# Layer norm of the first layer shared between two engines, small weights loaded later

## What is computed

```python
def reference(L0_attn_x, ...):
    x = x + 0.5 * ffn(layernorm(x), gate_W, w1_e, w3_e, w2_e, w1_s, w3_s, w2_s)   # layer 1
    x = x + attn(layernorm(x), w_qkv, w_swiglu, w_out)
    x = x + 0.5 * ffn(layernorm(x), ...)                                          # layer 2
```

## Time and profile before

| | |
|---|---|
| median of 3 executions | 735.5 us (734.17 to 737.56) |
| span of the profiled execution | 733.5 us |
| TensorE busy | 660.3 us, 90% |
| VectorE busy | 458.8 us, 63% |
| ScalarE busy | 411.3 us, 56% |
| GpSimd busy | 430.6 us, 59% |

### The profile page before, as it was taken

How to read it: one execution, slowest core, us unless ns; L and a number is a source line. 1 busy time by engine, 2 the same in 40 slices (tenths; PEclk the granted TensorE clock), 3 DMA queues, 4 the chain that set the end, 5 groups by cost and what they waited for, 6 DMA issues and landing times.

```text
span 733.5 us, 14294 instructions
## 1 busy us (share of the span) xinstructions
PE 660.3 (90%) x4860; PEld 602.1 (82%) x4860; DVE 458.8 (63%) x1177; ACT 411.3 (56%) x861; POOL 430.6 (59%) x511
## 2 busy tenths in 40 slices
PE   3878999999999999957987777999999999999995
PEld 3767879999999999825654574888999999999983
DVE  6678895554445555359999867884555555544536
ACT  2658617666666666236654436664666666666520
POOL 5600075777777776489987424007577777777530
PEclk9989999999999999989999997999999999999999
DMA  9542011221222231131100002402212212212137
GB/s 296 231 78 40 1 42 38 56 52 52 52 55 52 52 53 44 57 105 44 47 12 1 0 1 46 73 2 49 40 55 54 52 52 56 51 53 52 43 104 261
DMA packets 35685, 45.91 MB, mean 63 GB/s; under 512 B 6432, under 2 KB 27936, under 8 KB 35232
## 3 DMA queue, kind: packets, MB, share of 16 engines
q1 hardware_dynamic: 25632, 24.39, 11.8%
q0 software_dynamic: 9984, 20.63, 11.5%
HBM read 28.41 MB, written 16.58 MB: 61 GB/s over the span
## 4 chain that ended last, share of the span: by engine, by line
PE 65%; DVE 20%; issue 4%; ACT 4%; POOL 3%; DMA 2%; SPq 1%; ACTq 0%; POOLq 0%; DVEq 0%
PE psY L1487 18%; PE psG L1334 6%; PE psU L1336 6%; PE psG L1336 6%; PE psU L1335 6%; PE psG L1335 6%; PE psU L1334 6%; PE psH L1405 4%; DVE rec L1076 3%; PE psT L1433 2%; DVE hs L748 2%; DVE XN L738 2%; DVE ln_stats L725 1%; DVE xn L1060 1%; POOL results L641 1%
## 5 line engine op out<-in xcount | busy, mean ns | idle before, releaser
L626 POOL DMA_INDIRECT rows<-tokens,source x156 | 153.7, 985 | 156.3 <-DVE source L900 98.6
L1155 ACT ACTIVATE silu<-psG 128x512 f32<-128x512 f32 x220 | 131.1, 596 | 150.6 <-PE psG L1336 147.2
L954 DVE TENSOR_TENSOR hT<-silu,psU 128x512 f32<-128x512 f32 x156 | 107.4, 688 | 158.9 <-PE psU L1336 150.3
L641 POOL DMA_INDIRECT results<-yout,target x156 | 153.8, 986 | 63.3 <-issue 45.7
L1487 PE MATMUL psY<-W,hT 128*128 x1232 | 162.4, 275 | 1.8 <-DVE yout L980 1.8
L1487 PEld LDWEIGHTS psY<-W,hT 128*128 128x128 f32 x1232 | 150.4, 191 | 2.2 <-DVE hT L954 2.2
L1229 ACT ACTIVATE w_high<-W13H 128x1024 fp32r x78 | 82.7, 1061 | 59.0 <-PE psU L1336 54.8
L1334 PE MATMUL psG<-xTH,w_high 128*128 128x256 f32 x312 | 100.0, 321 | 0.7 <-ACT w_low L1229 0.7
L1336 PE MATMUL psG<-xTH,w_low 128*128 128x256 f32 x312 | 88.0, 282 | 0.0
L1336 PE MATMUL psU<-xTH,w_low 128*128 128x256 f32 x312 | 88.0, 282 | 0.0
L1335 PE MATMUL psU<-xTL,w_high 128*128 128x256 f32 x312 | 87.7, 281 | 0.0
(11 more groups left out here) (188 smaller groups left out, 1215.7 us busy)
## 6 DMA issues: line engine op xcount, KB each, us to landing
W<-w_e SPq DMA_DIRECT2D x3, 2048.0 KB, 13.7
tokens<-XN SPq DMA_DIRECT2D x16, 260.0 KB, 5.9
Y<-results SPq DMA_DIRECT2D x32, 128.0 KB, 2.2
YF<-results SPq DMA_DIRECT2D x16, 256.0 KB, 5.9
rows<-tokens,source POOLq DMA_INDIRECT x156
results<-yout,target POOLq DMA_INDIRECT x156, 2.3
X<-x SPq DMA_DIRECT2D x8, 256.0 KB, 5.5
out<-X SPq DMA_DIRECT2D x8, 256.0 KB, 2.8
```

Of the source, the lines that this page charges most:

```text
L626: pool.indirect_dma_start(rows[:, slot(l, g), t, :], None, tokens, bass.IndirectOffsetOnAxis(ap=source[:, tile:tile + 1], axis=0))\
L641: pool.indirect_dma_start(results, bass.IndirectOffsetOnAxis(ap=target[:, tile:tile + 1], axis=0), yout[:, g % 2, t, :], None).then_inc(y_ ...
L954: dve.tensor_tensor(hT[:, s.u // PT % 2, half, :].rearrange("p f c -> p (f c)"), silu[:, s.u % 2, :], psU[:, s.u % 2, :], ALU.mult).then_i ...
L1155: act.activation(silu[:, s.u % 2, :], psG[:, s.u % 2, :], ACT.Silu).then_inc(silu_done, 1)
```

## The change

Three things change, all for layer 1 only. VectorE normalises the first two of a chunk's four tiles, and ScalarE the other two as `Identity(scale * x + bias)`, with `ln_rstd` as scale and a new `ln_shift = -mean * rstd` as bias. For that VectorE makes `ln_minus` (minus the mean, one more small operation in each `stats`) and GpSimd multiplies it by `ln_rstd` (one more small operation in each `scale_ln`). The small weights are issued behind the fourth transfer of `X` in place of the second. TensorE no longer waits for `small_in` ahead of its first transpose but ahead of its first gate product, and ScalarE makes `W13SH` at c = 3 in place of first. The core of the diff:

```diff
+LN_DVE = CH // 2
@@ SyncE
-                if c == 1:
+                if c == 3:
                     for dst, src in ((GATE[:, :], gateT), (W13S[:, 0, :], w1_s), (W13S[:, 1, :], w3_s),
@@ SyncE, keep_tokens
+                    if l == 0:
+                        sp.wait_ge(xn_half_done, s.i + 1)
@@ GpSimd, scale_ln
                 pool.wait_ge(ln_stat, s.i + (l * CHUNKS + 1))
+                if l == 0 and s.i >= 2:
+                    pool.wait_ge(xn_half_done, s.i - 1)
                 pool.tensor_tensor(ln_rstd[:, s.u, :], ln_var[:, s.u, :], minus_half[:, 0:CH], ALU.pow)\
                     .then_inc(ln_scaled, 1)
+                if l == 0:
+                    pool.wait_ge(ln_scaled, s.i + 1)
+                    pool.tensor_tensor(ln_shift[:, s.u, :], ln_minus[:, s.u, :], ln_rstd[:, s.u, :], ALU.mult)\
+                        .then_inc(ln_shifted, 1)
@@ VectorE, stats
+                if l == 0:
+                    if s.i >= 2:
+                        dve.wait_ge(ln_shifted, s.i - 1)
+                    dve.tensor_scalar(ln_minus[:, s.u % 2, :], ln_mv[:, s.u % 2, :, 0], -1.0, None, ALU.mult)
@@ VectorE, normalise
-                for t in range(CH):
+                for t in range(LN_DVE if l == 0 else CH):
@@ ScalarE
-                if l == 0:
+                def normalise_half(c):
+
+                    act.wait_ge(ln_scaled, c + 1)
+                    act.wait_ge(ln_shifted, c + 1)
+                    for t in range(LN_DVE, CH):
+                        i = act.activation(XN[:, c * CH + t, 0:D], X[:, c * CH + t, :], ACT.Identity,
+                                           scale=ln_rstd[:, c % 2, t:t + 1], bias=ln_shift[:, c % 2, t:t + 1])
+                    i.then_inc(xn_half_done, 1)
+
+                def split_shared():
                     act.wait_ge(small_in, 64)
                     act.activation(W13SH[:, :, :], W13S[:, :, :], ACT.Copy).then_inc(ws_high, 1)
                 if l == 0:
+                    normalise_half(0)
                     for c in range(CHUNKS + 2):
+                        if c == 3:
+                            split_shared()
+                        if c < CHUNKS - 1:
+                            normalise_half(c + 1)
                         if c < CHUNKS:
                             copy_xnT(Step.of(c, 2))
@@ TensorE
             pe.wait_ge(consts, CONSTS)
-            pe.wait_ge(small_in, 64)
@@ TensorE, ahead of the transposes of chunk c
                         pe.wait_ge(xn_done, CHUNKS * l + c + 1)
+                        if l == 0:
+                            pe.wait_ge(xn_half_done, c + 1)
@@ TensorE, ahead of the gate products of chunk c - 1
                         pe.wait_ge(xnT_done, CHUNKS * l + c)
+                        if l == 0 and c == 1:
+                            pe.wait_ge(small_in, 64)
```

More of the change, by code:

```diff
@@ L225, in macaron @@
         ln_rstd = sb("ln_rstd", [P, 2, CH])
+        ln_minus = sb("ln_minus", [P, 2, CH])
+        ln_shift = sb("ln_shift", [P, 2, CH])
         row_a = sb("row_a", [P, TILES])
@@ L367, in macaron @@
         ln_scaled = sem("ln_scaled")
+        ln_shifted = sem("ln_shifted")
         xn_done = sem("xn_done")
+        xn_half_done = sem("xn_half_done")
         xnT_psum = sem("xnT_psum")
```

## The result

The changed kernel takes 736.26 us (median of 20 executions, 734.17 to 738.19) against 734.96 us of the kernel before (20 executions, 733.47 to 737.56). The ratio is 1.0021, with a 95% interval of 1.0011 to 1.0030: 1.5 us more (0.8 to 2.2); the two medians themselves lie 1.3 us apart. It was forecast as 736.4 us, within 0.5% of no change. Its profiled execution spans 735.0 us against 733.5.

The account below looks back on a forecast made before the run. The front up to `hs(3)` was taken to bound the kernel, with T(7) passing shifts on one to one. T(7) +1.3 us, or +0.45 with an earlier upper clock, gave +0.9: 734.4 span, 736.4 us median, range 733.5 to 739.5.

Parts of the forecast that it names:

- The stall on X: VectorE's 1.7 us wait for the third chunk of X, behind 832 KB of small weights, was to go.
- ScalarE's half: Two normalises per chunk on ScalarE: 0.6 us of its time, 0.7 to the end, table load of 1.28 moved to 7.0.
- `W13SH` at c = 3: GpSimd's `low_shared` waits for it ahead of `scale_ln(4)`, putting the power of chunk 4 at 19.5, 2.5 us later.
- s: The start of `W13SH` on ScalarE behind `XNTH(0)`, forecast at 15.98 us.
- GpSimd the bound at 2.65 us a chunk: From c = 4 on, power, small product and `XNTL` were to give GpSimd a 2.65 us period, against 2.42 before.
- the port: A GpSimd `XNTL` holds up VectorE's `tensor_scalar` until it ends; with this rule ignored, +0.95 us in place of +1.3.
- The clock: TensorE without early gaps might reach its upper level sooner, L(1) ending 0.85 us earlier: +0.45 in place of +1.3, taken as +0.9.
- rival B: TensorE's idle stretch lowers its clock for c = 5 to 7; slower only from the second step; 738.5 to 740.6 us; chance 0.18.
- Sum: 733.5 + 0.9 = 734.4 us of span, plus 2.0 us to the median: 736.4 us, +0.1%.
- Rival C: ScalarE's `normalise_half(7)` between `silu(0)` and `silu(1)` costs two table loads, +1.3 to +2.6 us, 737.7 to 739 us; chance 0.1.
- Rival A: The front's gain comes through if GpSimd and ScalarE meet `W13SH` sooner, -0.9 to 0, 734.6 to 735.5 us; with D 0.22.

Follow-up runs that it names:

- e1: The changed kernel with `W13SH` made on ScalarE at c = 1 in place of c = 3; ratio to the kernel before 0.9979.
- e10: The changed kernel with VectorE normalising all four tiles (no half on ScalarE) and `W13SH` made at c = 1; ratio to the kernel before 0.9977.
- e2: The changed kernel with only the order of transfers and waits changed, VectorE normalising all four tiles; ratio to the kernel before 1.0050.
- e5: The changed kernel with 22 unused products of constants on TensorE ahead of its wait for chunk 4; ratio to the kernel before 1.0025.
- e6: e1 with unused products of constants on TensorE, 9 ahead of the wait of chunk 4 and 4 ahead of chunk 5; ratio to the kernel before 0.9974.
- e9: The changed kernel run and profiled once more, unaltered; ratio to the kernel before 1.0017.
- e8: e1 with GpSimd's `XNTL` one chunk later in layer 1, behind the power of chunk 5; ratio to the kernel before 0.9962.
- e7: e2 with 23 unused products of constants on TensorE ahead of the wait of chunk 4; ratio to the kernel before 1.0049.
- e11: e8 with `normalise(7)` ahead of `hs(0)` on VectorE and `normalise_half(7)` ahead of `silu(0)` on ScalarE; ratio to the kernel before 0.9964.

## Why the prediction was right, point by point

**The stall on X goes, and VectorE gets ahead.** Right: no wait for X, `stats(2)` at 7.41; `ln_var(4)` in the forecast at 12.8, in the trace at 12.74. The third X landed at 6.75, not 5.4, still 0.7 us ahead of its use.

**ScalarE's half.** The size was at my upper bound, not in the middle: one instruction with two pointers took 0.482 us, a pair 0.88 to its end (I took 0.7, the bound was 0.87). The 387 ns quoted in the prediction beside the row are for a form with one pointer, and the kernel's has two. The table load moved to 7.07 and T(0) to 9.38, where I had 9.05.

**`W13SH` at c = 3 and GpSimd's queue.** The step that decided, and right: GpSimd idle 3.98 us ahead of `W13SL`, the power of chunk 4 straight behind it. I had s at 15.98, or 15.1 if TensorE's upper level came early; measured 15.18 and 15.97. e1 and e10 show by undoing it that the delay is this wait, and e2, which has the wait without the half, is late too. With the clock kept up in both, 3.37 us at the power of chunk 4 come through to `hs(3)` as 3.35 us (e5 against e6, 36.13 and 32.78).

**GpSimd the bound at 2.65 us a chunk, and the port.** Right in kind, too large in size. The powers stand 2.47, 2.68 and 2.71 us apart: GpSimd's own cycle is 2.47, and ahead of the later two it waits 0.17 us for an `ln_var`, which the blocked `ln_minus` made late, so that between the powers of chunks 4 and 6 the chain goes over VectorE. From `ln_shift(4)` to `ln_shift(6)` it is 5.18 us in the first profile and 5.19 in e9, and I had 5.65. The blocked operations came where they were forecast: the second of `normalise(4)`, until 21.19, and `ln_minus(6)`, 1.18; one more, `ln_minus(7)`, 0.90. So the rule of the Trainium skill (SBUF — State Buffer, section Who interferes with whom) held in this case for `W13SL` and `XNTL`. In e8, where no `XNTL` runs beside `normalise(4)`, 1.55 becomes 0.60. For the power it did not hold: in the kernel before, four normalises took their usual 1.11 us beside the one at 16.99:

```profile
16.82 1.11 DVE L738 TENSOR_SCALAR XN<-X,ln_mv,ln_rstd 128x128 f32<-128x128 f32 x4
```

**The clock.** I took half of a gain of 0.85 us for an earlier upper level. In the first profile L(1) did run at it (1.13 us), in e9 only in part (1.44): the halving was a fair guess. Against that stood rival B, which I gave 0.18: a lower level behind the idle stretch. It happened in both profiles of the changed kernel, granted 0.50 and 0.69 at 20 to 24 us, and cost 0.4 us at `hs(3)` in the first and nothing in e9, because, as B's text has it, ScalarE's chain covers most of the first step. From S(0) on TensorE ran at the upper level, so the second step, from which B was to decide, was not touched. One reading there was loose: the idle stretch of the earlier trace rows does not precede the 10 us but lies in them (TensorE idle 4.71 us until 46.41, then 0.43 us for a product).

**Sum.** +0.9 us forecast at the front; +0.58 and +0.95 measured in two profiles against the first one of before. Part of the agreement is two errors that cancel: GpSimd's stretch was 0.47 us shorter than forecast, and ScalarE's from `ln_shift(6)` to the end of `silu(0)` 4.36 us in the first profile and 3.96 in e9, where I had 3.65. That the median of 736.26 lies 0.1 us under the forecast is luck: the 735.5 us from which I started was a median of three, and twenty executions give 734.96, so the shift was 1.3 to 1.5 us and not 0.9, and some 0.5 us of it isn't seen in the front. Rival C (table loads) did not come: no load stands between `silu(0)` and `silu(1)`. Rival A (gain comes through) needed what e1 makes: `W13SH` early.

## What to carry to other kernels

When a step is moved later on one engine, read on every other engine what is queued behind the wait for it, not only who uses its result: here a product that nobody needed for another 8 us (`W13SL` done at 18.65, S(0) at 26.52) stood ahead of a small power that everybody needed. A gain in front of such a wait is given back at it. And an order that leaves a matmul engine idle for a few microseconds may have to be paid once more, in its clock, as soon as that engine is the bound.

## What the runs showed of the hardware

- TensorE's granted clock fell to 0.50 in a gap of 5.2 us, at about 19.5 us in one profile of the changed kernel and at 21.5 in the other, and in e1 behind a single gap of 2.18 us; with products of constants in the gap (e5, e6, e7) it stayed at 1.00. A gap of 1.85 us at the same place in e11, and the gaps of up to 1.4 us between 16 and 31 us in the kernel before, left it at 1.00.
- At the start of the kernel the granted clock reads 1.00 while groups take 1.11 and 1.92 us and later 0.66 and 1.06: there the durations tell the level, not the clock's column. When the upper level is reached differs between executions of one program: T(3), behind L(1), began 0.8 us apart in two profiles of the changed kernel.
- A `tensor_scalar` of VectorE on four elements took 1.18 us in place of 0.17 beside a GpSimd `tensor_tensor` of 128x512, and `bn_stats`, `bn_aggr` did not lengthen beside one (0.86, 0.38). Beside the power of GpSimd (1.03) four normalises took their usual 1.11 us.
- An ACTIVATE of 128x128 with scale and bias pointers took 0.482 us, against 0.365 with a scale pointer alone; that row reads its input from PSUM and this one from SBUF, so the difference isn't the pointer's alone for certain.
